# A fused gated-attention kernel on one core: weighing the values of all 16 heads in one block a batch, with 16 places for transposed probabilities

## What is computed

```python
def attention(q, k, v):            # q = layernorm(x); k = v = ctx; S = 256, H = 16, D_K = 32
    query, key_, value = (heads(a @ w.T + b) for a, w, b in ...)
    scores = einsum('bhqd,bhkd->bhqk', query, key_) / sqrt(D_K)
    attn = softmax(where(causal, scores, -inf))
    x = einsum('bhqk,bhkd->bhqd', attn, value)
    return merge_heads(x) @ w_o.T + b_o

x = x + tanh(g_xattn) * attention(layernorm(x), ctx, ctx)
x = x + tanh(g_ffn) * (dequantised(quantised(layernorm(x))) @ dequantised(quantised(weight)).T + bias)
```

## Time and profile before

| | us |
|---|---|
| median of 3 runs | 1403.73 |
| lowest and highest of them | 1403.28, 1406.11 |
| the profiled execution | 1401.43 |
| its span in the trace | 1399.5 |

### The profile page before, as it was taken

One profiled execution on the slowest core, in us unless ns is written; L12 is line 12 of the kernel. 1 busy time (PEld: TensorE's weight loads), 2 busy tenths in 40 slices (PEclk: granted clock), 3 DMA queues, 4 the chain that ended last, 5 costly groups with the idle time before them and its releaser, 6 DMA issues.

```text
span 1399.5 us, 35240 instructions
## 1 busy us (share of the span) xinstructions
PE 1365.1 (98%) x10856; PEld 1217.4 (87%) x10856; DVE 1084.8 (78%) x4219; ACT 895.9 (64%) x2969; POOL 866.5 (62%) x1387
## 2 busy tenths in 40 slices
PE   7899999999999999999999999999999999999987
PEld 6788988888888898988889988889998888998865
DVE  6777778877778877778877778878778878778774
ACT  5567666666666666666666666576666566666562
POOL 2456665566665566666566666566666566666564
PEclk9999999999999999999999999999999999999998
DMA  8444434444434444434444434444434444434320
GB/s 265 104 122 114 110 95 115 120 130 116 109 93 117 119 131 116 107 95 119 119 129 118 112 90 118 120 126 121 111 90 119 118 125 123 110 90 120 87 70 31
DMA packets 156616, 159.11 MB, mean 114 GB/s; under 512 B 28688, under 2 KB 131088, under 8 KB 156432
## 3 DMA queue, kind: packets, MB, share of 16 engines
q1 hardware_dynamic: 156432, 156.88, 42.4%
HBM read 39.33 MB, written 16.78 MB: 40 GB/s over the span
## 4 chain that ended last, share of the span: by engine, by line
PE 91%; DVE 3%; SPq 2%; issue 1%; DMA 1%; POOL 1%; ACT 1%; DVEq 0%; ACTq 0%; POOLq 0%
PE proj L517 20%; PE proj L519 20%; PE proj L518 20%; PE pT_ps L578 12%; PE proj L594 6%; PE proj L621 5%; PE s_ps L567 4%; PE s_ps L568 2%; SPq L360 2%; DMA q_stack<-q_hi 0%; DMA bias_v<-in_L_xattn_b_v 0%; DVE all_probs L843 0%; ACT all_probs L697 0%; DMA k_stack<-k_lo 0%; DVE stats L851 0%
## 5 line engine op out<-in xcount | busy, mean ns | idle before, releaser
L435 POOL TENSOR_TENSOR all_probs<-all_probs,rden 128x128 f32<-128x128 f32 (+1 forms) x1024 | 517.5, 525 | 446.8 <-DVE rden L901 445.3
L697 ACT ACTIVATE all_probs<-all_probs,neg_max 128x128 f32<-128x128 f32 (+1 forms) x1024 | 458.8, 451 | 375.9 <-DVE neg_max L843 375.7
L843 DVE CUSTOM_DVE_ANT_0 all_probs<-s_ps,causal 128x128 f32<-128x128 f32 (+1 forms) x1024 | 323.4, 353 | 195.2 <-PE s_ps L568 189.3
L578 PE MATMUL pT_ps<-ident,all_probs 128*128 128x128 f32 x1536 | 263.7, 281 | 8.5 <-ACT all_probs L774 4.2
L697 ACT ACTIVATION_READ_ACCUMULATOR all_probs<-all_probs,neg_max 128x1 f32 x1024 | 195.4, 191 | 0.0
L970 DVE COPY all_probs<-pT_ps 128x384 f32<-128x384 f32 x256 | 139.2, 544 | 53.7 <-PE pT_ps L578 53.5
L578 PEld LDWEIGHTS pT_ps<-ident,all_probs 128*128 128x128 f32 x1536 | 160.0, 142 | 23.4 <-issue 12.5
L567 PE MATMUL s_ps<-k_stack,q_stack 96*128 96x256 f32 x512 | 154.1, 301 | 4.1 <-DVE neg_max L843 2.6
L517 PE MATMUL proj<-cT_hi,wk_hi 128*128 128x256 f32 x512 | 153.7, 300 | 3.4 <-DVE cT_lo L895 1.8
L517 PE MATMUL proj<-aT_hi,wq_hi 128*128 128x256 f32 x512 | 147.8, 289 | 1.2 <-DVE aT_lo L895 1.2
L518 PE MATMUL proj<-cT_lo,wk_hi 128*128 128x256 f32 x512 | 142.7, 279 | 0.0
(11 more groups left out here) (116 smaller groups left out, 3459.5 us busy)
## 6 DMA issues: line engine op xcount, KB each, us to landing
k_stack<-k_hi SPq DMA_DIRECT2D x512, 64.0 KB, 2.0
q_stack<-q_hi SPq DMA_DIRECT2D x512, 64.0 KB, 2.1
cs<-in_ctx SPq DMA_DIRECT2D x32, 512.0 KB, 6.3
xs_yz<-in_x SPq DMA_DIRECT2D x32, 512.0 KB, 4.5
k_stack<-k_lo SPq DMA_DIRECT2D x256, 64.0 KB, 2.0
q_stack<-q_lo SPq DMA_DIRECT2D x256, 64.0 KB, 2.1
out<-xs_yz SPq DMA_DIRECT2D x64, 256.0 KB, 2.3
vs<-in_L_xattn_w_k SPq DMA_DIRECT2D x2, 512.0 KB, 5.5
```

The source lines that it names most:

```text
L435: last = nc.gpsimd.tensor_tensor(p, p, rden[:, sd, t, h:h + 1].to_broadcast([P, (1 + t) * P]), ALU.mult)
L578: last = nc.tensor.transpose(pT_ps[h % 2][:, m * P:(m + 1) * P], probs[:, h % P_RING, m * P:(m + 1) * P], ident[:, :])
L697: last = nc.scalar.activation(probs[:, h % P_RING, cols], probs[:, h % P_RING, cols], ACT.Exp, scale=-1.0, bias=neg_max[:, sd, t, h:h + 1] ...
L843: last = nc.vector.tensor_tensor_reduce(probs[:, h % P_RING, cols], s_ps[h % 2][:, cols], causal[:, (1 - t) * P:], 1.0, MASKED, ALU.add, A ...
```

## The change

Both blocks of values of a batch now stand one behind the other in slot 3 of step `i`, for batch `i-3`, between the scores and the transposes of that slot; the block in slot 11 is gone. `probsT` has 16 places, so a copy waits for the block of the batch before. On DVE the results of units and `output_lo` now stand in front of the normal rows and the copy; on ACT the copy stands in front of the exponentials. `SLOT_PARTS` moves parts between slots: the last part of the first half of `k` goes from slot 3 to slot 2 (and so is taken out in slot 3, not 4), and from slot 10 on each unit moves by a part or so.

```diff
-AV_SLOTS = (11, 3)
-AV_STEPS = (2, 3)
+AV_SLOT = 3
+AV_STEPS = 3
-SLOT_PARTS = (2, 4, 4, 1, 1, 5, 4, 2, 3, 4, 4, 1, 3, 3, 3, 2)
+SLOT_PARTS = (2, 4, 5, 0, 1, 5, 4, 2, 3, 4, 3, 3, 3, 3, 2, 2)
...
-        all_probs = sb("all_probs", [P, P_RING + AV_HEADS, 3 * P])
+        all_probs = sb("all_probs", [P, P_RING + HEADS, 3 * P])
...
-            def weigh_values(b, r, sd):
-                pe.wait_ge(pT_even, 8 * b + 4 * r + 4)
-                pe.wait_ge(pT_odd, 8 * b + 4 * r + 4)
+            def weigh_values(b, sd):
+                pe.wait_ge(pT_even, 8 * b + 8)
+                pe.wait_ge(pT_odd, 8 * b + 8)
                 pe.wait_ge(left["v"], 2 * b + 2)
-                free_bank("av", r, b)
-                bank = bank_of("av", r, b)
...
+                for r in range(2):
+                    free_bank("av", r, b)
+                    bank = bank_of("av", r, b)
...
+                    last.then_inc(av_done, 1)
...
+                    if live(b) and h % 2:
+                        act.wait_ge(pT_done, HEADS * b + h + 1)
+                        if some(b):
+                            act.wait_ge(av_done, 2 * (b - 1) + h // AV_HEADS + 1)
+                        nc.scalar.activation(probsT[:, h, :], pT_ps[1][:, 0:3 * P],
+                                             ACT.Copy).then_inc(pT_odd, 1)
                     if live(i - 2):
                         exponentials(i - 2, s, side(ph, 2))
...
                         reciprocals(i - lag, h, side(ph, lag))
+                    for kind, half, of in finished(i, s):
+                        unit(kind, half, of)
+                    if s == AV_SLOT + 1 and live(i - AV_STEPS):
+                        for r in range(2):
+                            output_lo(i - AV_STEPS, r)
                     if s in XN_SLOTS and i > 1 and live(i - 1):
                         normal_rows(i - 1, XN_SLOTS.index(s))
                     lag, b, h = transposed_head(i, s)
                     if live(b) and h % 2 == 0:
                         dve.wait_ge(pT_done, HEADS * b + h + 1)
...
-                    for kind, half, of in finished(i, s):
-                        unit(kind, half, of)
```

More of the change, by code:

```diff
@@ L117, in fused_kernel @@
         for s in range(SLOTS):
-            taken += [("av", r, i - AV_STEPS[r]) for r in range(2) if s == AV_SLOTS[r] and live(i - AV_STEPS[r])]
+            if s == AV_SLOT and live(i - AV_STEPS):
+                taken += [("av", r, i - AV_STEPS) for r in range(2)]
             taken += [(kind, half, b) for kind, half, b, part in work.get((i, s), ()) if part == 0]
@@ L580, in transpose_probs @@
                 last.then_inc(pT_done, 1)
-            def weigh_values(b, r, sd):
-                pe.wait_ge(pT_even, 8 * b + 4 * r + 4)
-                pe.wait_ge(pT_odd, 8 * b + 4 * r + 4)
+            def weigh_values(b, sd):
+                pe.wait_ge(pT_even, 8 * b + 8)
+                pe.wait_ge(pT_odd, 8 * b + 8)
                 pe.wait_ge(left["v"], 2 * b + 2)
-                free_bank("av", r, b)
-                bank = bank_of("av", r, b)
[L590 to L599, removed]
+                for r in range(2):
+                    free_bank("av", r, b)
+                    bank = bank_of("av", r, b)
+                    for half in range(2):
+                        for kt in range(T):
+                            for j in range(GROUP):
+                                h = AV_HEADS * r + GROUP * half + j
+                                last = nc.tensor.matmul(
+                                    bank[j * DK:(j + 1) * DK, half * S + kt * P:(half + 1) * S],
+                                    vs[:, sd, kt, h * DK:(h + 1) * DK],
+                                    probsT[:, h, 2 * P * kt:2 * P + P * kt], start=kt == 0,
+                                    stop=kt == T - 1, tile_position=(0, j * DK))
+                    last.then_inc(av_done, 1)
             def unit(kind, half, b, part):
@@ L657, in step @@
                         scores(i - 2, s)
-                    for r in range(2):
-                        if s == AV_SLOTS[r] and live(i - AV_STEPS[r]):
-                            weigh_values(i - AV_STEPS[r], r, side(ph, AV_STEPS[r]))
+                    if s == AV_SLOT and live(i - AV_STEPS):
+                        weigh_values(i - AV_STEPS, side(ph, AV_STEPS))
                     lag, b, h = transposed_head(i, s)
@@ L761, in step @@
                         unit(kind, half, of)
[L762 to L766, removed]
+                    if s == AV_SLOT + 1 and live(i - AV_STEPS):
+                        for r in range(2):
+                            output_hi(i - AV_STEPS, r)
                     lag, b, h = transposed_head(i, s)
```

14 lines of the change are left out of this document (5 added, 9 removed).

## The result

| | kernel before | changed kernel |
|---|---|---|
| median of the runs | 1403.80 us (4 runs, 1403.28 to 1406.11) | 1427.39 us (4 runs, 1421.62 to 1429.27) |
| ratio | | 1.0153, 95% interval 1.0136 to 1.0170 |
| profiled execution, span | 1401.43, 1399.5 us | 1429.27, 1427.5 us |

The change made the kernel 1.5% slower by the ratio; the medians lie 23.6 us apart and the two spans 28.0 us. The direction was forecast; the time lies 14 us above the likeliest value and 5 us above the range.

A forecast was written before the change was run, and what follows sets the result against it. PE, busy throughout, bounds the kernel; 29 steps of 0.7 wait less 0.27 saved (+12.5), with -0.9, -1.6, -1.5 and +0.9, give +9.4, so 1413 us on the runs' median; 8-in-10 range 1398 to 1422.

The forecast's parts named there:

- K: Start of ACT's k_hi, counted into the step: forecast mean 11.0 us; PE doesn't wait if it is at most 10.25.
- Saving of the block, 0.27: Slot 3: joining both blocks of values saves PE one entry and exit, 0.27 us a batch, at least 0.21.
- Where PE waits, and for what: Slots 3 to 5: head 2's transposes, wanted 12.98 us into the step, wait for DVE's copy of head 0.
- The chain: From the start of k_hi: 0.87 to k_lo, 0.80 k_lo, 0.45 xn, 0.56 copy, 0.05 semaphore: K + 2.73.
- The mean wait, 0.7: PE ahead of head 2's transposes: 13 steps wait 1.29 us, 17 wait 0.34; 0.7 taken, ends 0.3 and 1.05.
- long issues of SP: Transfers of q and k: now and then one issue is 1.1 us longer, in 7 of 30 groups; adds 0.25 to mean K.
- The other signs: If right: PE idle 15 to 25 us ahead of head 2's transposes, steps about 42.2 us with spread, k_hi waiting nearly always.
- The ends: Program's ends: batch 0's step -1.6 us, batch 1's -1.5; batch 31's step and the last step together +0.9.
- The joint saves nothing: Rival: the block's second half waits for its bank or copies, so the 7.8 us are gone: 1421 us, chance 0.04.
- more waits behind the first: Rival: DVE and ACT late from slot 3 on, further bank or transfer waits, 0.4 us a step: 1425 us, chance 0.07.
- copy in time: Rival: K stays below 10.25 in nearly every step, so PE keeps the 0.27: 1393 us, chance 0.12.
- Orders and moved parts: Parts moved between slots cost nothing by themselves; ACT's copy ahead of its exponentials: nothing.

The follow-up runs named there:

- b_block: Kernel before plus only the joined block of 16 heads in slot 3 and its 16 places, parts and orders as before: 1420.11 us, ratio 1.0106.
- c_early_xn: Changed kernel, with k's stack transfers out of k_hi issued first, k_lo's last with their own semaphore, and xn ahead of k_lo in slot 3: 1398.03 us, ratio 0.9958.

## Why the prediction was off

The step that failed is the price of the wait: the mechanism was forecast and came, but its mean was put at 0.7 us a step where 0.98 was measured, because K came later than forecast, with a tail that had been folded into a mean, and PE waited from an earlier K on. And the sum had no term for the clock that a long wait costs (4.8 us) and had both ends of the program too cheap (4.4 us). Point by point, in its own order.

- **Saving of the block, 0.27.** Right: 0.28 in b_block, and 0.25 kept in c_early_xn.
- **Where PE waits, and for what.** Right: head 2's transposes, for the copy of head 0, behind k_lo, k_hi and the landing. The chain holds link by link up to the end of the copy; the transposes start at K + 2.82 instead of K + 2.73. The second block adds the forecast 1.30 to slot 3.
- **The mean wait, 0.7: mis-sized.** It is 0.98 in 30 steps, which, with 0.25 saved for 0.27, makes 8.3 us over 29 steps. K's mean was 11.13 instead of 11.0, and PE waits from K = 10.18 on, not 10.25; I had also rounded 0.75 down. The typical step was right (0.66). What was missing is a tail: seven steps of 1.4 to 2.7 us. I had folded the long issues of SP into a shift of 0.25 of the mean; in the trace after they come together with landings of up to 4.2 us behind the last issue, where 2.0 is usual. The tail was there to be read before: in the trace of the kernel before, eight of the 30 landings of this last transfer took 2.8 to 4.0 us, which the median of 2.0 doesn't show. In the step of batch 7, SP (a long issue among q's, then k's last, then the next batch's x):

```profile
325.85 1.02 SPq L361 DMA_DIRECT2D q_stack<-q_lo  x1
...
329.72 1.22 SPq L361 DMA_DIRECT2D k_stack<-k_hi  x2
...
336.74 0.60 SPq L361 DMA_DIRECT2D k_stack<-k_lo  x1
337.38 0.59 SPq L386 DMA_DIRECT2D xs_yz<-in_x  x1
```

  The last k_lo, issued at 336.74, landed at 340.96. The Trainium skill, DMA: Bandwidth & Descriptors (Anatomy of one DMA), gives 2.0 us and the time of the bytes for a transfer issued from GpSimd, which for 64 KB makes an estimate of 2.15 us. The transfers here are issued from SyncE, and their median is 2.0. What cost PE is not the median alone: the seven long waits are 14 of the 29 us.
- **The clock: missing.** No term stood for it; three steps, 4.8 us. Together with the ends it also hid the saving in the row that was to show it: PE's busy time rose from 1365.1 to 1374.2 us instead of falling by 8. From the scores of batch 2 to those of batch 31 it is 1213.1 us before, 1216.1 in the changed kernel and 1206.8 in c_early_xn, where the saving shows. The other signs came as named: k_hi waits in every step, PE idles ahead of head 2's transposes (25.7 us in this view, just over the forecast 15 to 25), the steps spread.
- **The ends: -3.1 and +0.9 forecast.** The tail came to +2.9. In the ten kernels with the joined block it is 70.9 to 72.5 us, in the four without it 68.5 to 70.3, so this is no chance: the last batch's block, 64 matmuls, now lies alone in the last step, and PE's mean granted clock from the scores of batch 31 on is 0.87 where it was 0.93. That the block is the cause is argued from this, not tested by a run. The head came to -0.7. It can't be judged: over all kernels here the scores of batch 2 begin between 114.6 and 122.1 us, more apart than the term.
- **"The joint saves nothing" and "more waits behind the first".** Both were put aside with a sentence on one bank ("its bank held the second half of q"; "the bank is free at K + 1.7"). Both sentences are true of the changed kernel, because its copy waits longer than its banks. As an account of what the change is, they miss a point: the block makes the next takers wait for a younger one, and it is the moved part and the new order that give those banks back in time. So the copy couldn't be had in time by moving it: that gave 1426. The rival "copy in time" named steps of 41.55 us and 1393 us; c_early_xn, where k_hi doesn't wait for the last landing, has 41.57, and 1398 with 4.8 us of waits left and its ends dearer than forecast.
- **Orders and moved parts, taken to cost nothing by themselves.** Orders: right. Parts: wrong, +45 us without the orders.

The sum put right: the forecast's +9.4, +8.3 for the wait and the saving, +4.8 for the clock, +2.0 for the tail, +2.4 for the head, +1.3 for the wait on q's stack and -0.2 for the stall that is gone are the 28.0 us between the spans.

The cause of the late landings stays open. No run took the load of x away from behind the last transfer of k; its issue followed 0.64 us behind in the steps that landed in time too, and some steps with a long issue landed in time.

## What to carry to other kernels

When buffers go round in turn, a step that takes two where it took one makes the takers of the next turn wait for a younger one: write down who empties what, for that turn, before pricing an order. A wait that hangs on a transfer is to be priced by its spread and not by its median, and here it was cheaper to cut the chain behind the landing (transfer first what is overwritten first, and let only the last reader wait) than to reorder the engine in front of it. Parts of a change that pay for each other can't be priced one by one; the three here gave +15, -2 and +45 us alone and +24 together.

## What the runs showed of the hardware

- Behind a wait of about 2 us in the middle of dense work PE may run part of what follows at 1.2 GHz, for 1.6 us more. In the slot looked at, all 22 such falls in three kernels lay behind an idle time of 1.94 us or more, and 20 idle times as long had none. By these numbers, as an estimate, a wait that grows from 1 to 2.5 us can cost 3.1.
- One transfer of 64 KB, usually landed 2.0 us behind its issue, took 3.1 to 4.2 us in seven of 30 steps of the changed kernel (in one of them its own issue was long, 1.7 us): the last of k's twelve. The kernel before has eight of 2.8 to 4.0 us.
- Now and then an issue on SP takes 1.0 to 1.8 us instead of 0.6: in 26 of 30 groups of 24 (q's first half and k's second) in the changed kernel, in 20 of 30 before, there up to 2.0.
